# Tables of block numbers as 2-byte integers in a graph-convolution and mixture-of-experts kernel

## The reference

```
seg  = dst * 8 + etype
sums = segment_sum(x[src], seg)                 # one sum per node and edge type
mean = sums / max(count, 1)
out  = x @ Wroot + b + einsum('nrd,rde->ne', mean, W)
```

## Time and profile before

| what | value |
|---|---|
| median of three runs | 3063.42 us |
| span of the profiled execution | 3064.4 us |
| PE busy | 2352.2 us, 77% of the span |
| POOL busy | 1836.5 us, 60% |
| DVE busy | 1782.2 us, 58% |
| ACT busy | 1167.6 us, 38% |

### The profile page before, as it was taken

One profiled execution on the slowest core, in us unless ns is written; L12 is line 12 of the kernel. 1 busy time (PEld: TensorE's weight loads), 2 busy tenths in 40 slices (PEclk: granted clock), 3 DMA queues, 4 the chain that ended last, 5 costly groups with the idle time before them and its releaser, 6 DMA issues.

```text
span 3064.4 us, 82720 instructions
## 1 busy us (share of the span) xinstructions
PE 2352.2 (77%) x19212; PEld 1776.0 (58%) x19213; DVE 1782.2 (58%) x4944; ACT 1167.6 (38%) x2306; POOL 1836.5 (60%) x1908
## 2 busy tenths in 40 slices
PE   1456777778888887456777888888987189999999
PEld 0123444555666775123445556667776178888888
DVE  7434445555566664333445555656666278877777
ACT  5001223334445553011223344455542165655554
POOL 1777777766666553777777777666536623333333
PEclk9556789999999998557899999999995599999999
DMA  7343333333333321333343444333335432322222
GB/s 244 100 130 105 108 108 108 109 101 99 97 94 93 90 88 58 106 99 115 115 119 118 123 122 125 112 113 111 106 110 192 146 123 86 100 72 72 72 72 61
DMA packets 164416, 331.14 MB, mean 108 GB/s; under 512 B 35518, under 2 KB 101786, under 8 KB 164216
## 3 DMA queue, kind: packets, MB, share of 16 engines
q0 software_dynamic: 90864, 245.38, 26.9%
q1 hardware_dynamic: 39608, 41.02, 4.5%
q10 hardware_dynamic: 33872, 43.92, 4.5%
HBM read 283.29 MB, written 49.07 MB: 108 GB/s over the span
## 4 chain that ended last, share of the span: by engine, by line
PE 48%; POOL 24%; issue 15%; DVE 7%; DMA 3%; DVEq 2%; ACT 1%; POOLq 0%; SPq 0%; ACTq 0%
POOL ring L450 20%; PE more_banks L1254 15%; PE sum_banks L1392 8%; PE sum_banks L1234 7%; PE sum_banks L1235 5%; PE sum_banks L1382 4%; PE more_banks L1382 4%; POOL lot_in L470 3%; PE more_banks L1246 3%; DMA ring<-table,row_tab 2%; DVE sel L890 1%; DMA out<-edge_work,lot_ids 1%; PE more_banks L1366 1%; DVEq L881 1%; DVE weights L1072 0%
## 5 line engine op out<-in xcount | busy, mean ns | idle before, releaser
L450 POOL DMA_INDIRECT ring<-table,row_tab x1568 | 1509.2, 963 | 703.8 <-issue 339.0
L1254 PE MATMUL more_banks<-weights,stage 128*128 128x256 f16 x5292 | 846.9, 283 | 7.8 <-ACT stage L561 4.5
L589 ACT ACTIVATE stage<-sum_banks,inv 128x256 f16<-128x256 f32 x784 | 327.4, 471 | 815.5 <-DVE inv L923 398.7
L1254 PEld LDWEIGHTS more_banks<-weights,stage 128*128 128x128 f16 x5292 | 502.4, 101 | 144.9 <-issue 71.6
L1234 PE MATMUL sum_banks<-ring,sel 128*128 x1568 | 449.3, 287 | 161.1 <-DVE sel L890 84.2
L898 DVE TENSOR_SCALAR sel_more<-lane,win_off,key_tab 128x128 f16 x780 | 268.8, 345 | 443.4 <-SPq L355 371.2
L1234 PE MATMUL sum_banks<-ring,sel_more 128*128 x780 | 244.3, 314 | 350.0 <-DVE sel_more L898 193.8
L890 DVE SCALAR_TENSOR_TENSOR sel<-lane,win_off,key_tab 128x256 f16<-128x256 f16 x792 | 349.4, 482 | 240.4 <-PE more_banks L1254 235.8
L1235 PE MATMUL sum_banks<-ring,sel 128*128 x1568 | 448.7, 287 | 0.0
L561 ACT ACTIVATE stage<-more_banks 128x1024 f16<-128x1024 f16 x392 | 402.7, 1027 | 15.1 <-PE more_banks L1246 14.9
L1234 PEld LDWEIGHTS sum_banks<-ring,sel_more 128*128 x780 | 78.4, 100 | 529.7 <-issue 524.9
(11 more groups left out here) (287 smaller groups left out, 2763.0 us busy)
## 6 DMA issues: line engine op xcount, KB each, us to landing
ring<-table,row_tab POOLq DMA_INDIRECT x1568
weights<-L_ffn_W ACTq DMA_DIRECT2D x96, 178.5 KB
stage<-L_ffn_W ACTq DMA_DIRECT2D x16, 1024.0 KB, 5.5
edge_work<-lot_in SPq DMA_DIRECT2D x54, 260.0 KB, 2.7
table<-edge_work SPq DMA_DIRECT2D x7, 896.0 KB, 4.4
table<-edge_work ACTq DMA_DIRECT2D x49, 128.0 KB
out<-acc SPq DMA_DIRECT2D x6, 1024.0 KB
acc<-x SPq DMA_DIRECT2D x6, 896.0 KB, 11.0
```

The lines of the kernel that those rows point to most:

```text
L450: pool.indirect_dma_start(ring_rows[:, b % RING, 0:2 * D], None, tables[layer], bass.IndirectOffsetOnAxis(row_tab[:, b:b + 1], 0)).then_in ...
L589: act.activation(mean16[:, slot, h, 0:D], ps_sum[slot][h][:, 0:D], ACT.Copy, scale=inv[:, ds(c * 2 + h, 1)]).then_inc(mean_high[layer], 1)
L1254: return [pe.matmul(ps_out[par], rows[:, xp * KD + k, :], w16[:, wp, k, r * D:(r + 1) * D], start=part == 0 and n == 0, stop=part == PARTS ...
```

## The change

The three tables become uint16 in place of int32. Nothing else is edited: the instructions of every engine are the same and stand in the same order. A load of 20 numbers from `meta` reads 40 consecutive bytes in place of 80, one of 16 from `free_meta` 32 in place of 64, one of 4 from `lot_meta` 8 in place of 16. The copies and scans by which DVE writes the tables convert float32 to uint16 in place of int32, and three fills (lines 855, 856 and 991) cover half the bytes. The largest numbers that the tables can hold are 784 in the first column of `meta` and in the second, 784 + 3 * 392 = 1960 in `free_meta`, and 8 * 6528 = 52224 in `lot_meta`. `trips`, a single int32 number that four engines load once, stays as it is. Later tensors in SBUF start at addresses lower by 1616 bytes behind `meta` and by 3168 bytes behind `free_meta`.

```diff
-    f32, f16, i32 = mybir.dt.float32, mybir.dt.float16, mybir.dt.int32
+    f32, f16, i32, u16 = mybir.dt.float32, mybir.dt.float16, mybir.dt.int32, mybir.dt.uint16
...
-        meta_row = sb("meta", [1, 2 * (WINDOWS + 12)], i32)
+        meta_row = sb("meta", [1, 2 * (WINDOWS + 12)], u16)
         meta = meta_row[:, :].rearrange("o (w c) -> o w c", c=2)
-        free_meta = sb("free_meta", [1, BLOCKS], i32)
+        free_meta = sb("free_meta", [1, BLOCKS], u16)
...
-        lot_meta = sb("lot_meta", [1, X + 1, 4], i32)
+        lot_meta = sb("lot_meta", [1, X + 1, 4], u16)
```

## The result

The changed kernel takes 3478.23 us (median of four runs, 3476.89 to 3480.49), the kernel before 3064.16 us beside it: ratio 1.1347 [1.1331, 1.1363], 414 us slower. The likeliest case, no change, and the whole range were wrong.

What follows compares the result with a forecast made beforehand. It saw no single bound: POOL's gathers pace each layer's start, PE the later part. 63 exposed PE loads times 0 ns, with all other terms 0, left 3063 us; range 3022 to 3072 us.

Steps and rivals of the forecast that it cites:

- The likeliest case: All table loads: price per number, so durations and the span stay, 3063 us (3059 to 3068), chance 0.56.
- I take the price per number: Register loads on PE, DVE and SP: a 2-byte number costs one read like a 4-byte one, so durations stay.
- The slope of 64 ns: PE's loads: 4 numbers take 333 ns and 20 take 1361, so 64 ns for each further number.
- The upper bound: PE's loads: two reads per 2-byte number, 128 ns, add 1.28 us per load, 81 us in PE's stretches: 3144 us.
- my own sum: PE's tile starts where PE sets the pace: 63 exposed loads times the change per load, taken as 0 ns.
- The second rival: Line 1227 in PE's 63 tiles: 2-byte numbers cost more to read, 3071 us up to 3144; dearer loads, chance 0.17.
- The rows of lines 881 and 359 have to move by the same factor: A sign: the loads at these lines change duration by the same factor as line 1227.
- DVE would hide its own longer load: DVE's loads from 608 to 1197 us: DVE waits 176.2 us for PE in 36 tiles, 4.9 us per tile.
- PE's wait in POOL's stretches is hidden by POOL: 95 to 608 and 1352 to 1885 us: POOL's gathers set the pace, so longer PE waits do not move the end.
- the writing of the tables: DVE's copies, 354 ns for 392 numbers: at most part of about 2 us in all, fills less; taken as 0.
- the moved addresses: Lower addresses of other tensors change no instruction: 0 us.

Runs made afterwards that it cites:

- g1: The control with 36 more SP register loads before the first expert, three per form: twelve 4-byte numbers took 764 ns from the tile's start, 2975 starting two in.
- g2: The control with such SP loads in the opposite order, plus 3 and 6 numbers: eight 4-byte numbers took 523 ns starting four in, 1674 starting two in.
- d3: DVE alone loads from a 2-byte copy of `meta`, against the control: 3426.61 us, +197 us.
- e4: The changed kernel with DVE's load again from a 4-byte table, masked on DVE: 3496.03 us, ratio 1.1403 to the kernel before.
- d2: PE alone loads from a 2-byte copy of `meta`, against the control: 3615.15 us, +386 us.
- the control: The kernel before with 4-byte tables, its compared numbers and the experts' lot numbers masked with `& 0xFFFF`: 3229.12 us, ratio 1.0538 to the kernel before.

## Why the prediction was wrong

**The step that failed** is "I take the price per number". I argued that a load which collects no neighbours at 4 bytes has no reason to collect them at 2. It does collect them at 4 bytes, four at a time, as far as the counts and starts of g1 and g2 show, and not at 2. The slope of 64 ns was a fourth of a read of some 250 ns: 4, 8, 16 and 20 numbers, all of the earlier trace rows, are multiples of four and start at one, so the straight line through them could not show it. A hint was in the trace all along: the single number of `trips` takes 492 ns on PE, which is more than four numbers of `lot_meta` (333).

**The upper bound** of two reads per number, 128 ns, came from the same slope and was too low by nearly half; 234 ns were measured. With 3.37 us in place of 0 my own sum would have given 63 * 3.37 = 212 us, against 414 measured; the clock and the stretches of POOL, below, make up most of the rest. The second rival had the sign right and the place in part, and its price was too small.

**"The rows of lines 881 and 359 have to move by the same factor"** held: 3.3 and 3.35 beside 3.48 on line 1227.

**"DVE would hide its own longer load"** was wrong. 4.9 us per tile is a sum over four waits, and only the one at the load can be used (d3, +197 us). Beside PE's longer load nothing of it is seen: undoing it gained nothing (e4).

**"PE's wait in POOL's stretches is hidden by POOL"** held for no stretch: 114 us. PE's load alone (d2) makes the same 13 and 22 tiles 45 and 71 us longer than in the control, so it is PE's wait that comes through, although POOL no longer sets the pace alone in the control, whose first stretch is 561 us long in place of 513. POOL as the bound held only while stands were short beside what the ring covers.

**A term that was missing**: the clock. At the tile shown the clock is down to 0.50 for some 3 us after a stand of 4.01 us, and PE's busy time is 98 us longer in all. After the old 0.65 us it was not: the clock is 1.00 on both sides.

**Costed at nothing**: the writing of the tables, rightly, by its rows (377 beside 354 ns), and the moved addresses, of which no row shows a cost and which no run changes alone. The rest of the kernel, from the last tile's load on, grew by 10.8 us (799.9 to 810.7), and the experts' loads are in that.

**The rule of the Trainium skill**, page "Runtime: NRT & Kernel Launch", section "Instruction fetch mechanics", gives about 200 ns per register. I read its form, a price per register, as support for no change and set its figure aside as another memory's. The measured 200, 221 and 234 ns per 2-byte number agree with the figure, though these numbers come from SBUF; the 64 ns of an aligned 4-byte number do not.

## What to carry to other kernels

Tables that an engine reads into registers should stay 4-byte, consecutive, start at a multiple of four numbers and be read in multiples of four; the smaller type saves nothing there, and a load of 20 numbers takes 3.5 times as long. A price found from a slope holds for the counts and forms in the rows only: where all counts are multiples of one number, a step between them stays hidden. Slack that a view sums over a tile must be looked up at the instruction that is to use it, and what a longer stand costs must be read by stretch: the same DVE load cost 3.7 us per tile in one layer and 0.9 in the other.

## What was not expected of the hardware

- Aligned groups of four 4-byte numbers cost about as much as one number of any other form: 523 ns for 8, against 1674 for 8 two numbers later, and about 1000 for 4 that are 2 bytes wide or taken every second one.
- The granted clock fell from 1.00 to 0.50 just after a stand of 4.01 us, while PE was busy again, and not after one of 0.65 us.
- Masks are not free: one register operation more per compared number costs 5.4% in the control (+164 us).
- The same kernel took 3064 us in some groups and 3455 to 3509 in others, and 3064 and 3455 both stand under the same chip number. In the groups with the longer time some register instructions show 0.7 us; why is open.
